# Cross-attention and expert feed-forward on one core: one GpSimd subtraction moved behind the join of the sums, and the loop over head pairs written out

## What is computed

```python
def xattn(x, context, Wq, Wk, Wv, Wo, bo):             # 16 heads of 64
    q, k, v = x @ Wq, context @ Wk, context @ Wv       # split into heads
    scores = einsum('bqhd,bkhd->bhqk', q, k) / 8
    out = einsum('bhqk,bkhd->bqhd', softmax(scores), v)
    return out.reshape(B, Nq, 1024) @ Wo + bo
x = x + xattn(layernorm(x), ctx, ...)
x = x + ffn(layernorm(x), ...)   # 8 experts, each takes its 513 tokens of highest router score:
                                 # gelu(tokens @ w1 + b1) @ w2 + b2, times the score, added to its tokens
```

## Time and profile before

| what | value |
|---|---|
| three runs, us | 1369.89, 1369.21, 1369.24 (median 1369.24) |
| the profiled execution, us | 1360.78 |
| its span, us | 1359.0 |
| granted TensorE clock, mean over the span | 0.974 of full |
| busy: TensorE / VectorE / ScalarE / GpSimd, us | 1281.1 / 1025.0 / 808.7 / 907.9 |
| first and last place where a row maximum is taken off (L847), us | 76 and 998 |

### The profile page before, as it was taken

How to read it: one execution, slowest core, us unless ns; L and a number is a source line. 1 busy time by engine, 2 the same in 40 slices (tenths; PEclk the granted TensorE clock), 3 DMA queues, 4 the chain that set the end, 5 groups by cost and what they waited for, 6 DMA issues and landing times. The chain is left out here.

```text
span 1359.0 us, 25161 instructions
## 1 busy us (share of the span) xinstructions
PE 1281.1 (94%) x8436; PEld 802.6 (59%) x8436; DVE 1025.0 (75%) x1708; ACT 808.7 (60%) x1092; POOL 907.9 (67%) x464
## 2 busy tenths in 40 slices
PE   6999999999999999999999999999998916999996
PEld 5655555555455555555455555455447916999996
DVE  5778877887887888788778877878987775666652
ACT  4566666666665666666666666666664214657653
POOL 2357877987887788788778877977696003345453
PEclk8999999999999999999999999999999957999998
DMA  9520010001001000200110020012314442554422
GB/s 281 212 102 17 17 57 17 17 25 58 17 24 45 32 17 20 62 17 25 38 39 17 17 65 17 17 35 92 113 33 152 141 138 79 145 132 113 105 38 27
DMA packets 76441, 88.86 MB, mean 65 GB/s; under 512 B 11387, under 2 KB 56220, under 8 KB 76316
## 3 DMA queue, kind: packets, MB, share of 16 engines
q1 hardware_dynamic: 69532, 78.32, 17.7%
q0 software_dynamic: 6784, 8.94, 4.1%
HBM read 58.13 MB, written 27.99 MB: 63 GB/s over the span
## 5 line engine op out<-in xcount | busy, mean ns | idle before, releaser
L932 POOL TENSOR_TENSOR acc_p<-acc_p,x_in 128x1024 f32<-128x1024 f32 x192 | 489.0, 2547 | 120.9 <-ACT x_in L1029 113.2
L112 DVE TENSOR_REDUCE mx_part<-ps_m 128x1 f32<-128x512 f32 x521 | 344.7, 686 | 163.9 <-PE ps_m L81 162.6
L1029 ACT ACTIVATE x_in<-ps_s 128x1024 f32<-128x1024 f32 x384 | 380.7, 1024 | 100.4 <-PE ps_s L847 71.1
L861 PE MATMUL ps_o<-x_in,v 128*64 128x512 f32 x1664 | 406.2, 606 | 0.0
L836 PE MATMUL ps_s<-q,k 64*128 64x512 f32 x2496 | 384.5, 394 | 1.5 <-ACT x_in L1029 1.5
L836 PEld LDWEIGHTS ps_s<-q,k 64*128 64x128 f32 x2496 | 268.8, 184 | 46.4 <-ACT x_in L1029 8.1
L81 PE MATMUL ps_m<-k,q 64*128 64x512 f32 x736 | 208.6, 453 | 8.4 <-DVE mx_part L112 3.5
L861 PEld LDWEIGHTS ps_o<-x_in,v 128*64 128x64 f32 x1664 | 99.5, 136 | 181.1 <-issue 141.2
L81 PEld LDWEIGHTS ps_m<-k,q 64*128 64x128 f32 x736 | 97.6, 183 | 155.3 <-issue 110.6
L713 ACT ACTIVATE kept<-ps_m 128x512 f32<-128x512 f32 x215 | 128.4, 597 | 82.4 <-PE ps_m L81 81.0
L932 DVE TENSOR_TENSOR acc_d<-acc_d,x_in 128x1024 f32<-128x1024 f32 x96 | 165.9, 1729 | 5.3 <-ACT x_in L1029 4.9
(11 more groups left out here) (251 smaller groups left out, 1913.2 us busy)
## 6 DMA issues: line engine op xcount, KB each, us to landing
w_in<-in_w SPq DMA_DIRECT2D x16, 1024.0 KB, 5.7
v_st<-rec_scr SPq DMA_DIRECT2D x64, 128.0 KB, 2.9
o_scr<-v_st SPq DMA_DIRECT2D x32, 256.0 KB, 2.1
v<-v_scr SPq DMA_DIRECT2D x7, 832.0 KB, 5.4
v_scr<-c_in SPq DMA_DIRECT2D x10, 512.0 KB, 3.5
c<-o_scr SPq DMA_DIRECT2D x2, 1792.0 KB, 8.4
x_in<-in_x SPq DMA_DIRECT2D x4, 512.0 KB, 9.6
m_rows<-mx_t SPq DMA_DIRECT2D x128, 1.0 KB
```

Source lines behind the costliest of these rows:

```text
L112: dve.tensor_reduce(part[:, j // S.MF, j % S.MF:j % S.MF + 1], bank[:, 0:S.MC], AX.X, ALU.max).then_inc(done or G.rough_used[hd], 1)
L861: last = pe.matmul(ps_o[hd * HP:hd * HP + DH, :], v[b][:, s, hd * DH:(hd + 1) * DH], probs[:, g % RING, hd * QC:(hd + 1) * QC], start=(s = ...
L932: eng.tensor_tensor(acc, other, probs[:, (u * KT + t) % RING, :], ALU.add).then_inc(done, 1)
L1029: act.activation(probs[:, g % RING, :], ps_s[:, g % 2, :], ACT.Exp, bias=G.pad_bias[:, 0:1] if s == KT - 1 else 0.0, scale=SCALE).then_inc ...
```

## The change

It has two parts.

1. `DIFF_LO` gets a new kind of place, `BEHIND_JOIN`: the step stands right behind the join at the start of the unit. Block c = 1 uses it: its lower half (L812) stood at (1, 6), behind the last addition and the `norm` of unit 1 and ahead of the join of unit 2; it now stands behind that join. ScalarE's move of the 256 columns for the same block (`DIFF_KEEP`) goes from slot 0 to slot 2 of unit 2, where it stands ahead of the rounding of key block 2.
2. `all_pairs` has no hardware loop: a Python loop issues pairs 1 to 6 one after the other, with constant counts in all waits. The 3 turns x 2 pairs become 6 pairs of code on each of the five engines.

```diff
-DIFF_LO = ((1, 2), (1, 6), (2, 2), (3, 0))
-DIFF_KEEP = ((1, 8), (2, 0), (2, 8))
+BEHIND_JOIN = -1
+DIFF_LO = ((1, 2), (2, BEHIND_JOIN), (2, 2), (3, 0))
+DIFF_KEEP = ((1, 8), (2, 2), (2, 8))
@@ pool_pair
                 if not (first and u == 0):
                     pool_join(pool, (u - 1) % UNITS, unit - 1)
+                if (u, BEHIND_JOIN) in DIFF_LO and not last:
+                    pool_diff_lo(pool, DIFF_LO.index((u, BEHIND_JOIN)), 1 - b, p)
                 for k in range(NPL):
@@ all_pairs
             pair(eng, 0, 0, first=True)
-            with eng.Fori(0, NP // 2 - 1) as i:
-                pair(eng, 2 * i + 1, 1)
-                pair(eng, 2 * i + 2, 0)
+            for p in range(1, NP - 1):
+                pair(eng, p, p % 2)
             pair(eng, NP - 1, 1, last=True)
```

## The result

The changed kernel takes **1359.9 us** (median of six runs, 1358.62 to 1361.98), the kernel before takes 1369.97 us (median of six, 1369.21 to 1371.38). The ratio is 0.9928, 95% interval 0.9915 to 0.9941: **10.1 us, or 0.7%, faster** (8.1 to 11.6 by the interval). I had forecast 5.1 us.

The account below looks back on a forecast made before the run. TensorE's own work plus its few idle moments was taken to bound the attention. Branches 3.6 and lower half 1.5 us, registers and ScalarE's move nothing: 1369.24 - 5.1 = 1364.1 us, range 1360.8 to 1368.2.

Parts of the forecast that it names:

- The branches: Writing out the attention's pair loop removes two branches back on TensorE's path, 1.95 and 1.66 us, together 3.6 us.
- The registers: Constant counts instead of register computing in the looped pairs' units: taken as 0, at most 1.2 us.
- The lower half: Unit 2 of pairs 0 to 6: VectorE's sum and the join come earlier, TensorE's idle time goes; 1.5 us.
- My bound of 6.4 us: Upper bound for the lower half's gain, 7 x 0.91 us, if VectorE's lateness also slowed TensorE without visible idle time.
- ScalarE's move: Moved to slot 2 of unit 2, it costs nothing, ending some 0.2 us ahead of the rounding.
- ScalarE idle for GpSimd's lower half: Sign in the profile after that would prove the forecast wrong; ScalarE's move in unit 2 waits for the lower half.
- The 8.46 us: Whole kernel: unprofiled median stands this much above the profiled execution, unexplained by any row; taken as unchanged.
- The loop's gain alone: Rival: in unit 2 another wait of the same size replaces TensorE's 0.2 us; 1365.6 us, chance 0.17.
- The branch free or its gap elsewhere: Rival: branch costs little, gap at 432 us has another cause, the loop's part gives nothing; 1367.7 us, chance 0.08.
- ScalarE stuck behind the move: Rival: join not earlier, so ScalarE's move delays the rounding, 0.2 us more in seven pairs; about 1367 us, chance 0.04.
- Straight code fetched too late: Rival: instruction streams run dry at six boundaries between pairs 1 to 7, adding 10 us; 1374 us, chance 0.05.
- More than forecast: Rival: the registers' 1.2 us or part of the 6.4 us bound is gained in the attention; 1359 to 1362 us, chance 0.06.

Follow-up runs that it names:

- pe_loop: Changed kernel with the old hardware loop kept for TensorE alone, the other four engines written out; 1368.14 us, ratio 0.9951 to the kernel before.
- rest_loop: Changed kernel with TensorE written out and the old hardware loop kept for the four other engines; 1363.86 us, ratio 0.9924 to the kernel before.
- loop_b: Kernel before with only the pair loop written out, old order kept, in a repeat set; 1357.00 us, ratio 0.9960 to the kernel before.
- fourth series: Kernel before and changed kernel rerun beside a one-branch version and one with the experts' loops written out; before 1369.24 us, changed 1360.81 us.
- second series: Set running pe_loop, rest_loop and two order variants of the changed kernel against the kernel before, which took 1374.53 us and was not profiled.
- order_only: Kernel before with only the new order (lower half behind the join, ScalarE's move), hardware loop kept; 1358.58 us, ratio 0.9983 to the kernel before.

## Why the forecast was right, and where it was wrong

- **The branches (3.6 us).** Right in place and size: 3.7 us by the distances in the profile after, and TensorE's branch alone, as pe_loop and rest_loop show. Written out, the first unit of a pair became a little longer (29.94 us in pair 1 of loop_b, 29.88 in the kernel before), so that the attention of the loop alone gained 2.9 to 3.3 us. It is not TensorE's own straight code that does this: rest_loop has 29.87, and pe_loop, where the four others are straight, 29.94. The 108 ns of the page that I had weighed, "Advanced Engine Details and Errata" of the Trainium skill, would be 0.2 us for both branches (an estimate from that page), and the runs rule that out as the price of a branch back over a pair's code.
- **The registers (0).** Right. rest_loop, which still computes in registers on four engines, is as fast in the attention (913.99) as the kernel after (914.25 to 914.73).
- **The lower half (1.5 us).** The mechanism held row by row: sum at 1.21 us, join 2.81 us behind the unit's start (forecast 2.93), no idle time for L112. The term was mis-sized. I took TensorE's idle time, "since it is what rows show of TensorE", and the rows show more when their starts are read: 0.51 us a unit, 3.6 us. This is the step that failed. My bound of 6.4 us held.
- **ScalarE's move (0).** Right in cost, wrong in a detail: I had it ending 0.2 us ahead of the rounding, and it ends at it. My statement that ScalarE idle for GpSimd's lower half would prove me wrong was too strong; it was 0.54 us, ahead of an instruction that was early.
- **What the sum lacked.** The clock's fall behind the first branch. I had the clock's uncertainty only at the start of the experts, and took the gap's price from one profile, which shows full clock behind it. A fall is worth 1.6 to 2.1 us. In four of eight profiles it is there, which would make about 1 us of a mean (an estimate from these two).
- **The 8.46 us, taken as unchanged.** The late gelus may be 5.5 to 6.2 us of it, and 186.8 against 186.9 us in the fourth series show them unchanged. A fall of the clock, absent from the profile, would be 1.6 to 2.1 us, and that part goes with the branch. So the assumption that all of it stays had no ground.
- **The rest of the 10.1 us.** The terms are about 3.1 (loop) + 3.5 (order) as measured + 1 (clock) as estimated = 7.6 us. The four measured ratios of the whole change, 0.9928, 0.9963, 0.9936 and 0.9951, have a mean of 0.9945, which is also 7.6 us, but by the medians the four gains have a mean of 8.7 us, so the agreement is in part luck. The interval of the first measurement, 8.1 to 11.6 us, doesn't reach down to 7.6. Some 2.5 us of its 10.1 are thus not accounted for, as in the second series. Its runs of the kernel before have neither profiles nor clocks on record, and the cause stays open.
- **The rivals.** The loop's gain alone is ruled out by order_only's short unit 2. The branch free or its gap elsewhere is ruled out by the straight distances of 30.03 and 30.05. ScalarE stuck behind the move is ruled out by the rounding, which came 0.49 us earlier in its unit. Straight code fetched too late is ruled out too: no row marked "issue" at any of the six boundaries. "More than forecast" was the case that came, for one reason on my list (part of the 6.4 us), one that was not, and a part that stays open. I gave it 0.06. I had the bound of 6.4 us in the text and let the range stop at 1360.8; had I taken the gap in starts, the forecast would have been 1369.24 - 3.6 - 3.6 = 1362.0, still 2.1 us above the measured 1359.9.

## What to carry to other kernels

On a bottleneck engine whose instructions overlap, read a stall from the distance of starts and compare it with the same place where nothing waits; the idle time in brackets can be half of it. A subtraction on GpSimd that is early for nobody can lengthen an addition on VectorE by nearly its own length (0.91 us for 1.07 here), so put it behind the step for which GpSimd waits anyway. And a branch back on the bound engine costs its gap and, in some executions, a slower clock behind it; on the four engines with time to spare it cost nothing here.

## What the hardware showed that I had not expected

- The granted clock fell to 0.50 for 3 us and more behind an idle time of TensorE of 1.8 to 2.2 us at the first branch, in four profiles of eight, and not at the second branch, whose idle time was 1.4 to 1.6 us. It didn't fall behind 2.00 us at the first branch in pe_loop. Why it does in one execution and not in the next no row says.
- Six pairs of straight code took fewer instruction packets than three turns of two: 63 and 40 against 71 and 54.
- The same instructions of the experts' part took 181.2 us in some executions and 186.8 in others, whichever of the two attentions ran ahead of them, and 190.8 to 192.0 in the four profiles of another series.
